# A gated linear-attention block with a gated feed-forward: norm chains in a new order on three engines, and a finished row's mean and variance by ScalarE and GpSimd

## The reference

```python
q, k, v = x @ Wq, x @ Wk, x @ Wv                      # 16 heads of 8
gate = exp(log_sigmoid(x @ Wgk1 @ Wgk2 + bgk2) / 16)
state_t = state_{t-1} * gate_t + v_t k_t^T            # 8 x 8 per head
o_t = state_t q_t
o = layernorm(o) * gamma + beta
r = (o * silu(x @ Wg)) @ Wout
x2 = layernorm(x + r)
h = silu(x2 @ w1.T * s1) * (x2 @ w2.T * s2)           # 128 -> 512
h = gelu(h @ h1.T * s);  h = gelu(h @ h2.T * s)       # 512 -> 512, twice
out = layernorm(x2 + h @ w3.T * s3)
```

## Time and profile before

| what | us |
|---|---|
| median of 3 runs | 179.19 |
| lowest and highest | 178.98, 179.69 |
| the profiled execution | 179.29 |
| its span, first to last instruction | 177.5 |
| PE busy | 160.9 (91%) |
| DVE busy | 141.6 (80%) |
| ACT busy | 110.2 (62%) |
| POOL busy | 109.4 (62%) |

### The profile page before, as it was taken

One profiled execution on the slowest core, in us unless ns is written; L12 is line 12 of the kernel. 1 busy time (PEld: TensorE's weight loads), 2 busy tenths in 40 slices (PEclk: granted clock), 3 DMA queues, 4 the chain that ended last, 5 costly groups with the idle time before them and its releaser, 6 DMA issues.

```text
span 177.5 us, 2647 instructions
## 1 busy us (share of the span) xinstructions
PE 160.9 (91%) x778; PEld 119.3 (67%) x778; DVE 141.6 (80%) x306; ACT 110.2 (62%) x179; POOL 109.4 (62%) x97
## 2 busy tenths in 40 slices
PE   0899999999879999999899999989999999999980
PEld 0766657868657666877666778567666875887870
DVE  0689989968898997698999987999998895854062
ACT  4454889992147635478683508667935388995722
POOL 8705998969609689970577989609684420803132
PEclk9999999999999999999999999999999999999999
DMA  3999920244200000000000000000020000041112
GB/s 109 284 380 416 398 91 0 59 122 118 59 4 0 0 2 0 4 2 0 0 0 0 0 0 0 0 0 0 0 63 0 0 2 0 0 104 32 34 31 63
DMA packets 7455, 10.55 MB, mean 59 GB/s; under 512 B 753, under 2 KB 5394, under 8 KB 6930
## 3 DMA queue, kind: packets, MB, share of 16 engines
q1 hardware_dynamic: 6866, 7.50, 13.9%
q0 software_dynamic: 576, 2.88, 4.2%
HBM read 8.55 MB, written 1.84 MB: 58 GB/s over the span
## 4 chain that ended last, share of the span: by engine, by line
DVE 21%; PE 19%; issue 14%; ACT 6%; POOL 3%; DVEq 1%; POOLq 0%; ACTq 0%
DVE state L1097 6%; PE ffn L640 5%; PE ffn L631 4%; DVE f_lo L1196 3%; DVE y L1109 2%; PE att L564 2%; PE ffn L609 2%; ACT f_hi L917 2%; PE ffn L614 1%; ACT last_f L1053 1%; DVE x L1133 1%; POOL o_rstd L360 1%; PE att L537 1%; ACT f_hi L909 1%; DVE r_stats L1121 1%
## 5 line engine op out<-in xcount | busy, mean ns | idle before, releaser
L1097 DVE TENSOR_TENSOR_SCAN state<-gate,att 128x512 f32<-128x512 f32 x32 | 38.3, 1208 | 2.2 <-PE att L553 2.2
L382 POOL TENSOR_TENSOR f_lo<-full,f_hi 128x512 fp32r<-128x512 f32 x18 | 23.0, 1298 | 25.1 <-DVE full L1185 18.1
L917 ACT ACTIVATE f_hi<-ffn,vec_cols 128x512 fp32r<-128x512 f32 x24 | 16.5, 688 | 27.5 <-PE ffn L640 27.3
L631 PE MATMUL ffn<-f_hi,h_hi 128*128 128x512 f32 x96 | 28.1, 407 | 0.2
L640 PE MATMUL ffn<-f_lo,h_hi 128*128 128x512 f32 x96 | 26.1, 399 | 0.0
L341 POOL TENSOR_TENSOR u_tok<-kv_tok 128x1024 f32<-128x1024 f32 x12 | 25.6, 2141 | 0.1
L356 POOL TENSOR_TENSOR o_acc<-o_acc,y 128x512 f32<-128x512 f32 x16 | 20.7, 1293 | 7.6 <-DVE y L1109 7.5
L631 PEld LDWEIGHTS ffn<-f_hi,h_hi 128*128 128x128 f32 x96 | 17.6, 188 | 5.8 <-ACT f_hi L917 1.5
L553 PE MATMUL att<-ident,u_tok 128*128 128x128 f32 x128 | 19.3, 278 | 1.6 <-DVE state L1097 1.2
L640 PEld LDWEIGHTS ffn<-f_lo,h_hi 128*128 128x128 f32 x96 | 17.8, 188 | 3.7
L553 PEld LDWEIGHTS att<-ident,u_tok 128*128 128x128 f32 x128 | 15.4, 143 | 6.2 <-DVE state L1097 3.2
(11 more groups left out here) (182 smaller groups left out, 349.2 us busy)
## 6 DMA issues: line engine op xcount, KB each, us to landing
h_raw<-in_hT SPq DMA_DIRECT2D x2, 1024.0 KB, 12.3
h_hi<-in_hT POOLq DMA_DIRECT2D x2, 1024.0 KB, 12.2
x_tok<-in_x SPq DMA_DIRECT2D x4, 256.0 KB, 5.8
out<-out_tok SPq DMA_DIRECT2D x3, 256.0 KB, 2.3
w_raw<-in_w12T SPq DMA_DIRECT2D x1, 512.0 KB, 5.5
w_hi<-in_w12T POOLq DMA_DIRECT2D x1, 512.0 KB, 9.2
q_swap<-q_hi SPq DMA_DIRECT2D x3, 128.0 KB, 2.3
q_swap<-q_lo SPq DMA_DIRECT2D x3, 128.0 KB, 2.4
```

The source lines that it names most:

```text
L382: nc.gpsimd.tensor_tensor(lo[:, o], full_block(layer, o), hi[:, o].bitcast(F32), ALU.subtract).then_inc(pool_rested, 1)
L631: nc.tensor.matmul(bank[:], h_hi[:, layer - 1, c, tile(o)], src_hi[:, c], start=(c == 0), stop=False)
L917: nc.scalar.activation(hidden[layer][0][:, o], bank[:], ACT.Gelu, scale=scales[:, 1 + layer, o:o + 1]).then_inc(gelu_hi_ready, 1)
L1097: nc.vector.tensor_tensor_scan(state[:, k % 3], gate[:, b], A[2 + k % 2][:], 0.0, ALU.mult, ALU.add).then_inc(scanned, 1)
```

## The change

Four things are changed, all in the loop part:

- **DVE**: attention_end no longer does e_statistics and e_mean_and_variance for the row a - 2 (they stay for row 2, behind the loop), and its order after last_sums is now rest(f, 1, 2), o_token_stats, o_mean_and_variance, apply_gate, rest(f, 1, 3).
- **ACT**: two new helpers. e_sums(b) runs four Identity passes of 128x128 with an accumulator over the finished row, after the first pair of gelus of layer 1; e_squares(b) runs four Square passes with the negative mean as bias and an accumulator, after the last pair. Each pass waits for the one before by semaphore. out_normalise(b - 2) comes one pair of gelus later.
- **POOL**: e_minus_of makes the negative mean from the sums, in ffn_middle behind two rests and ahead of two outer products; e_var_of makes variance plus epsilon from the squares, and with e_rstd_of stands at the end of attention_end, behind both outer products and r_rstd.
- **PE**: transpose_u(a + 1, 0) comes before ffn_out_rest instead of behind it; transpose_o before center_o; transpose_x2 in the middle of ffn_out_hi.

```diff
@@ POOL
+            def e_minus_of(b):
+                pool.wait_ge(e_summed, TILES * (b + 1))
+                if b >= 1:
+                    pool.wait_ge(e_shift_ready, b)
+                nc.gpsimd.tensor_scalar(e_minus[:], e_total[:], -1.0 / HID, 1.0, ALU.mult,
+                                        ALU.mult).then_inc(e_minus_ready, 1)
+
+            def e_var_of(b):
+                pool.wait_ge(e_squared, TILES * (b + 1))
+                if b >= 1:
+                    pool.wait_ge(e_rstd_ready, b)
+                nc.gpsimd.tensor_scalar(e_var[:], e_square[:], 1.0 / HID, EPS, ALU.mult,
+                                        ALU.add).then_inc(e_var_ready, 1)
...
             def attention_end(a, tiles, last_tiles):
                 o_rstd_of(a)
-                if a >= 2:
-                    e_rstd_of(a - 2)
                 outer_products(a + 1, tiles)
                 r_rstd_of(a)
                 outer_products(a + 1, last_tiles)
+                if a >= 2:
+                    e_var_of(a - 2)
+                    e_rstd_of(a - 2)
...
                 rest(b, 1, 0)
                 rest(b, 1, 1)
+                if b >= 1:
+                    e_minus_of(b - 1)
                 if follows:
                     outer_products(b + 2, (0, 1))
@@ PE
             def first_layer(b, f, with_lo, follows):
                 if follows:
-                    transpose_u(b + 1, 0)
                     transpose_u(b + 1, 1)
...
                 ffn_hidden(f, 2, 0, with_lo)
+                transpose_o(a)
                 center_o(a)
-                transpose_o(a)
                 ffn_hidden(f, 2, 1, with_lo)
...
-                ffn_out_hi(f, with_lo)
+                ffn_out_hi(f, (0, 1), with_lo)
                 transpose_x2(a)
+                ffn_out_hi(f, (2, 3), with_lo)
+                if follows:
+                    transpose_u(a + 1, 0)
                 ffn_out_rest(f)
@@ ACT
+            def e_sums(b):
+                act.wait_ge(e_sum_ready, b + 2)
+                if b >= 1:
+                    act.wait_ge(e_minus_ready, b)
+                act.wait_ge(*rested(b + 1, 0, 2))
+                for j in range(TILES):
+                    if j >= 1 or b >= 1:
+                        act.wait_ge(e_summed, TILES * b + j)
+                    nc.scalar.activation(full[:, 2, 0:HID], out_tok[:, b, j], ACT.Identity,
+                                         accum_out=e_total[:, j:j + 1]).then_inc(e_summed, 1)
+
+            def e_squares(b):
...
+                for j in range(TILES):
+                    if j >= 1 or b >= 1:
+                        act.wait_ge(e_squared, TILES * b + j)
+                    nc.scalar.activation(full[:, 2, 0:HID], out_tok[:, b, j], ACT.Square, bias=e_minus[:, j:j + 1],
+                                         accum_out=e_square[:, j:j + 1]).then_inc(e_squared, 1)
...
-                for o in range(OB):
-                    ffn_gelu(b, 1, o)
-                    if o == 0 and b >= 2:
-                        out_normalise(b - 2)
+                ffn_gelu(b, 1, 0)
+                e_sums(b - 1)
+                ffn_gelu(b, 1, 1)
+                if b >= 2:
+                    out_normalise(b - 2)
+                ffn_gelu(b, 1, 2)
+                ffn_gelu(b, 1, 3)
+                e_squares(b - 1)
@@ DVE
-            def attention_end(a, f, e):
+            def attention_end(a, f):
...
                 read_out(a, 5)
-                if e is not None:
-                    e_statistics(e)
                 scan(a, 7)
...
                 rest(f, 1, 2)
+                o_token_stats(a)
+                o_mean_and_variance(a)
                 apply_gate(a)
-                o_token_stats(a)
                 rest(f, 1, 3)
-                o_mean_and_variance(a)
-                if e is not None:
-                    e_mean_and_variance(e)
```

More of the change, by code:

```diff
@@ L110, in gla_ffn_kernel @@
         e_rstd = sb("e_rstd", [P, TILES])
+        e_total = sb("e_total", [P, TILES])
+        e_square = sb("e_square", [P, TILES])
         A = [ctx.enter_context(nc.psum_tensor(f"att{i}", [P, L], F32)) for i in range(4)]
@@ L204, in gla_ffn_kernel @@
         e_sum_ready = sem("e_sum_ready")
+        e_summed = sem("e_summed")
+        e_squared = sem("e_squared")
         e_stats_ready = sem("e_stats_ready")
@@ L642, in ffn_hidden_rest, with ffn_out_hi @@
                 last.then_inc(hid_ready, 1)
-            def ffn_out_hi(b, with_lo):
-                bank_read(b, 2, 1)
-                for c in range(OB):
+            def ffn_out_hi(b, blocks, with_lo):
+                if 0 in blocks:
+                    bank_read(b, 2, 1)
+                for c in blocks:
                     pe.wait_ge(gelu_hi_ready, 2 * OB * b + OB + c + 1)
@@ L785, in rows @@
                 transpose_x2(0)
+                transpose_u(1, 0)
                 first_layer(0, None, with_lo, True)
@@ L932, in out_normalise @@
                                          bias=e_shift[:, j:j + 1]).then_inc(out_ready, 1)
+            def e_sums(b):
[9 more added lines that the diff above has]
+            def e_squares(b):
+                act.wait_ge(e_minus_ready, b + 1)
+                if b >= 1:
+                    act.wait_ge(e_var_ready, b)
+                act.wait_ge(e_summed, TILES * (b + 1))
+                for j in range(TILES):
[3 more added lines that the diff above has]
+                                         accum_out=e_square[:, j:j + 1]).then_inc(e_squared, 1)
             def sum_lo(n):
@@ L1210, in e_mean_and_variance @@
             def e_mean_and_variance(b):
-                mean_and_variance(b, e_stats, e_stats_ready, e_mv, e_mv_ready, e_var, e_var_ready)
+                dve.wait_ge(e_shift_ready, b)
+                mean_and_variance(0, e_stats, e_stats_ready, e_mv, e_mv_ready, e_var, e_var_ready)
                 nc.vector.tensor_scalar(e_minus[:], e_mv[:, :, 0], -1.0, 1.0, ALU.mult,
@@ L1329, in _ @@
             first_layer(0, None, True)
-            attention_end(1, 0, None)
+            attention_end(1, 0)
             with dve.Fori(0, B - 2) as i:
@@ L1336, in _ @@
                 first_layer(i + 1, i, True)
-                attention_end(i + 2, i + 1, i)
+                attention_end(i + 2, i + 1)
             make_x2(B - 1, B - 2)
@@ L1361, in _ @@
                 col = slice(j, j + 1)
-                seen = TILES * last + j + 1
+                seen = TILES + j + 1
                 dve.wait_ge(w3_ready, B + j)
```

## The result

The changed kernel takes 181.75 us (median of 4, 181.01 to 182.35) against 179.44 for the kernel before in the same round: ratio 1.0133, 95% interval 1.0089 to 1.0177. It is slower by 2.3 us. I had forecast slower by 1.2 to 1.3 (1.17 in the sum, 180.5 against 179.19), and 181.75 lies 0.5 above the upper end of my range. The profiled execution took 182.35, with a span of 180.6 against 177.5.

A forecast was written before the change was run, and what follows sets the result against it. Bound by a ring: DVE without a hole, then a chain across engines from projection to scan 0. Passes add +0.86, +0.25, +0.06 = +1.17 on 179.29: 180.46, forecast 180.5 us; likeliest case 179.9 to 181.1, overall range 177.6 to 181.2.

The forecast's parts named there:

- the hold: DVE's o_var waits until POOL's outer product ends, at most 1.35 and 1.42 us in loop passes 1 and 2; chance 0.56.
- Projection in pass 1: First loop pass: PE's projection of attention output o starts at 73.58 us instead of 71.46, waiting for gated o.
- a fee of 0.37: Rival: o_var loses only a fixed 0.37 us at each of two outer products; 178.4 us, chance 0.12.
- From the projection to scan 0: End of a row's attention, PE's projection to DVE's first scan of the next row: 9.32 us if u-transposes are ready.
- Pass 2: Second loop pass, to 115.7 us before: projection at 106.62, scan 0 at 115.94 against 115.69, +0.25 us.
- Pass 3: Last loop pass, no outer product beside o_var: projection at 138.83, ACT's x_hi ends at 146.84 against 146.78, +0.06 us.
- The sum: Three loop passes, +0.86, +0.25 and +0.06 us, tail untouched: +1.17 on the profiled 179.29, giving 180.46.
- No hold: Rival: o_var takes its 0.16 us under POOL's outer product; -1.60, so 177.7 us, faster; chance 0.22.
- ScalarE as the bound: Rival: ACT sums of 1.0 us each exceed 2.9 of cover, delaying layer 2; 181.6 us; chance 0.10 shared with late u-transposes.
- early transposes without effect: Rival: outer product late, scan 0 keeps 0.70 us idle in two passes; 181.9 at most; chance 0.10 shared with ACT.
- The gains: Early u-transposes remove 0.70 us before scan 0 in two passes; moved last-norm statistics give PE 0.12 in passes 2 and 3.

The follow-up runs named there:

- TensorE kept busy: Changed kernel plus seven discarded 128x512 matmuls ahead of the projection in passes 1 and 2: 181.18 us, ratio 1.0089 to the kernel before.
- the second chip: Changed kernel measured again, unaltered, on the chip of further experiments: 182.24 us, ratio 1.0141 to the kernel before, six executions of 181.35 to 183.00.
- the split of the outer products: Changed kernel with one GpSimd outer product ahead of o_rstd and two behind, instead of two and one: 178.24 us, ratio 0.9929 to the kernel before.

## Why the prediction was wrong, and where it was right

The sign and the hold were right; the size was about half of what was measured, and the lower clock behind the wait was not in the sum at all. Point by point:

- **Projection in pass 1: 73.58 forecast, 73.56 measured.** The whole chain of terms behind it held: 0.60 + 0.04 (transposes at 69.26, o_stats at 69.90), 1.45 (o_var at 71.35), and the hold taken whole, until 0.15 before the outer product ends, og at 72.77. The choice of a hold that lasts as long as GpSimd's operation, over a fee of 0.37, was the one that mattered, and 1.49 and 1.78 settle it. The Trainium skill says the same, page "SBUF — State Buffer", section "Who interferes with whom": the shared access is an exclusive lock, and whoever issued first has it for the whole instruction. The trace now agrees at the length in question, but for the last 0.14 us before the outer product's reported end.
- **From the projection to scan 0: 9.32 forecast, 11.00, 9.45 measured in passes 1 and 2. This is the step that failed.** I took the 9.32 from a pass in which TensorE came to the projection without a pause, and carried it over to one in which I had myself computed a pause of 2 us (71.46 to 73.58). About 0.12 of the excess is in both passes: a projection behind a wait takes 1.16 instead of 1.05. The other 1.55 of pass 1 is the clock. With TensorE kept busy the stretch measured 9.44. A hint was at hand, in the Trainium skill's page "TensorE: Matmul & The Clock Gate", Part 1: the array runs at one of two clocks, by how busy it has been. The windows agree on the two levels, with 1.00 and 0.50 of full speed. I had asked of every delay only who waits for it, never what the waiting engine loses by standing still.
- **Pass 2: +0.25 forecast, +0.48 measured** (scan 0 to scan 0: 34.13 against 33.65). The projection came 24.68 after scan 0, forecast 24.58; e_minus takes the 0.16 that I had put (104.13 to 104.29), but starts 0.09 after the rests end (101.49 plus 2.55, POOL L400). The remaining 0.13 is the 9.45 above.
- **Pass 3: +0.06 forecast, +0.19 measured** (118.69 to 149.97 against 31.09), again mostly the projection behind a wait.
- **The sum.** In the profiled execution +2.52, +0.48, +0.19, and -0.09 in the tail make the 3.1 by which the spans differ. Without the clock's 1.55 it would have been 1.5, inside my range. With TensorE kept busy the ratio is 1.0089, 1.6 us over the kernel before, with an interval that holds the 1.0073 I had forecast. But the clock is not all of the miss. The two executions of the first round whose mean clock is high took 181.01 and 181.44, on either side of my upper end of 181.2, and those on the second chip 181.35 and 181.99. So the clock, which comes and goes from execution to execution, took the median clear of the range; without it the time would have been about at the range's end. The 0.4 by which 1.5 exceeds my 1.17 is in the trace: 0.11 in pass 1, 0.23 in pass 2 and 0.13 in pass 3, less 0.09 in the tail, most of it the slower projection behind a wait. Between the 1.55 that the low stretch costs in the traced pass and the 0.9 between executions the record doesn't decide.
- **No hold, 177.7:** not what happened, but taking o_var away from VectorE gave 177.95, and the split of the outer products 178.24. The rival's price was right.
- **ScalarE as the bound, and early transposes without effect:** both excluded by the profile; 0.43 for a sum, and no idle left before scan 0.
- **The gains:** the sum had 1.4 us for the earlier transposes (0.70 in two passes), and of the moved last norm only 0.12 on TensorE in passes 2 and 3. On their own the two gave 1.0 and 0.6 us, and together in the old order 2.4. They were hidden in the changed kernel by a loss larger than they are: the new order alone costs 4 us.

Open is why 1.9 us of idle TensorE costs the clock in one execution and not in the next, at the same place of the program.

## What to carry to other kernels

Before a small VectorE operation with two SBUF inputs is put on the path, look at what GpSimd does at that moment: a 128x4 addition of 0.16 us was held here until the outer product it met was nearly over, 1.5 and 1.8 us in all, and moving either of the two away gained some 4 us. Undoing the reordering gained 5. When a sum contains a new wait of TensorE like the 1.9 us here, add the lower clock behind it as a term with a chance, and check in the windows whether the duration rows were taken with or without such a pause. A change of several edits that loses should be taken apart before it is dropped; here all but one part together gained 1.3%.

## What was not expected of the hardware

- An idle stretch of TensorE of 1.9 us was followed in both profiled executions of the changed kernel by some 3.4 us at half the clock, and in the profiled execution of the order alone by none. By the mean clocks, a weak witness, six of ten and two of four executions had it. In the traced pass it cost 1.55 us; executions with a low mean are 0.9 longer. One of 2.9 us was followed by the low clock in all three passes of the profiled execution, for 3.4, 6.8 and 6.8 us. Seven matmuls whose result is thrown away took less time than the wait.
- The hold of VectorE by GpSimd ends about 0.15 before the end of GpSimd's operation in the trace, and the held instruction ends 0.02 after it: 72.84 to 72.82, 108.52 to 108.50, 76.83 to 76.81. The old order with all other edits has a short one too, where nobody on the path waits for it: o_var of pass 2 takes 0.29, to 105.31, under an outer product that ends at 105.29.
- Accumulating on ScalarE is cheap: a 128x128 Identity with its accumulator read is 0.43 from start to start, the read 0.19 of it, although each waits for the one before.
